# Attention with a bias over 1024 positions: in steps with 3, 5 or 7 key blocks, the smaller group of blocks is worked first

## The reference

```python
x = x + layer0(x)   # attention: LN, q and k normalised, relative position bias, causal, null key
x = x + layer1(x)   # attention: LN, a given bias (16, 1024, 1024), key mask, causal, null key
x = x + moe2(x)     # 8 experts, top 2, and a shared expert
x = x + moe3(x)
# an attention layer, with b=2, n=1024, 16 heads of 64, one shared k and v for all heads:
sim  = q @ k.T + bias               # (b, h, n, n+1), causal and key mask applied
attn = softmax(sim)
out  = LN((attn @ v) @ Wout)        # 1024 -> 256
```

## Time and profile before

| what | value |
|---|---|
| median of 3 runs | 1618.56 us |
| the profiled execution | 1616.94 us |
| its span | 1615.1 us |
| TensorE matmul busy | 1434.6 us (89%) |
| VectorE busy | 1398.2 us (87%) |
| ScalarE busy | 1168.1 us (72%) |
| GpSimd busy | 903.7 us (56%) |
| the six steps T2, T4, T6, T10, T12, T14 | 74.8, 86.8, 93.4, 62.3, 75.9, 89.8 us |

### The profile page before, as it was taken

How to read it: one execution, slowest core, us unless ns; L and a number is a source line. 1 busy time by engine, 2 the same in 40 slices (tenths; PEclk the granted TensorE clock), 3 DMA queues, 4 the chain that set the end, 5 groups by cost and what they waited for, 6 DMA issues and landing times.

```text
span 1615.1 us, 45627 instructions
## 1 busy us (share of the span) xinstructions
PE 1434.6 (89%) x15680; PEld 1069.2 (66%) x15680; DVE 1398.2 (87%) x3629; ACT 1168.1 (72%) x3093; POOL 903.7 (56%) x1766
## 2 busy tenths in 40 slices
PE   4677778888999999977788999999999989999998
PEld 2455556666777777855666777777878756666665
DVE  6667888899999999977789998999999889888887
ACT  4566778888989999967788898989999633333332
POOL 6666778776756556577665344444343366632222
PEclk8789999999999999999999999999999999999999
DMA  6002211112222134012122122212223000000000
GB/s 158 18 28 69 71 48 54 60 67 73 80 87 93 48 107 131 9 47 67 54 61 79 60 75 87 84 68 88 100 106 106 2 27 20 1 1 1 14 14 27
DMA packets 49954, 96.50 MB, mean 60 GB/s; under 512 B 2922, under 2 KB 26560, under 8 KB 49728
## 3 DMA queue, kind: packets, MB, share of 16 engines
q1 hardware_dynamic: 48420, 92.93, 17.7%
q10 hardware_dynamic: 1308, 0.67, 0.2%
HBM read 91.41 MB, written 2.17 MB: 58 GB/s over the span
## 4 chain that ended last, share of the span: by engine, by line
PE 57%; DVE 20%; ACT 7%; issue 7%; POOL 4%; DVEq 0%; ACTq 0%; POOLq 0%
PE tp L1787 10%; DVE biased L1253 6%; PE sc L1655 6%; DVE p_lo L1351 5%; PE sc L1445 4%; PE sc L1447 4%; PE sc L1446 4%; PE sc L1656 4%; DVE q_a L1285 3%; PE aux L1445 3%; PE op L1445 3%; PE aux L1447 2%; PE aux L1446 2%; PE op L1447 2%; PE op L1446 2%
## 5 line engine op out<-in xcount | busy, mean ns | idle before, releaser
L1351 DVE TENSOR_TENSOR p_lo<-tp,p_hi 128x256 f16<-128x256 f32 (+3 forms) x896 | 424.8, 496 | 78.8 <-ACT p_hi L932 70.0
L1787 PE MATMUL tp<-ident,probs 128*128 128x128 f32 x2304 | 414.7, 280 | 24.6 <-DVE p_lo L1351 20.3
L932 ACT ACTIVATE p_hi<-tp 128x256 f16<-128x256 f32 (+3 forms) x896 | 385.2, 445 | 39.4 <-PE tp L1787 26.3
L832 ACT ACTIVATE probs<-biased,neg_max 128x256 f32<-128x256 f32 (+7 forms) x512 | 396.2, 774 | 14.7 <-DVE neg_max L1253 12.9
L1445 PE MATMUL op<-v_s,p_hi 128*128 128x64 f16 x2304 | 297.6, 194 | 28.2 <-DVE p_lo L1351 18.9
L1655 PE MATMUL sc<-k_a,q_a 128*128 128x512 f16 (+3 forms) x768 | 254.1, 331 | 65.9 <-DVE neg_max L1253 50.7
L1787 PEld LDWEIGHTS tp<-ident,probs 128*128 128x128 f32 x2304 | 261.6, 142 | 67.5 <-issue 29.0
L1446 PE MATMUL op<-v_s,p_hi 128*128 128x64 f16 x2304 | 297.2, 193 | 0.0
L1447 PE MATMUL op<-v_s,p_lo 128*128 128x64 f16 x2304 | 297.2, 193 | 0.0
L1445 PEld LDWEIGHTS op<-v_s,p_hi 128*128 128x128 f16 x2304 | 219.7, 99 | 47.7 <-DVE p_lo L1351 30.8
L1656 PE MATMUL sc<-k_b,q_b 128*128 128x512 f16 (+3 forms) x768 | 242.0, 329 | 0.0
(11 more groups left out here) (354 smaller groups left out, 3617.9 us busy)
## 6 DMA issues: line engine op xcount, KB each, us to landing
bias<-rel_table SPq DMA_DIRECT2D x4, 2048.0 KB, 9.1
bias<-in_fside_16xSxS SPq DMA_DIRECT2D x4, 2048.0 KB, 8.1
bias<-rel_table SPq DMA_DIRECT2D x4, 1792.0 KB, 7.3
bias<-in_fside_16xSxS SPq DMA_DIRECT2D x4, 1792.0 KB, 7.3
bias<-rel_table SPq DMA_DIRECT2D x4, 1536.0 KB, 6.2
bias<-in_fside_16xSxS SPq DMA_DIRECT2D x4, 1536.0 KB, 6.5
bias<-rel_table SPq DMA_DIRECT2D x4, 1280.0 KB, 5.6
bias<-in_fside_16xSxS SPq DMA_DIRECT2D x4, 1280.0 KB, 6.5
```

The lines of the kernel that those rows point to most:

```text
L832: ac.activation(probs[:, i % 2, 0:w], biased[:, i % 2, 0:w], ACT.Exp, bias=neg_max[:, u % 2, i % HU:i % HU + 1], scale=-1.0, accum_out=row ...
L932: ac.activation(p_hi[:, gi % 4, 0:nb * P], tp[gi % 2][:, 0:nb * P], ACT.Copy)\
L1351: ve.tensor_tensor(p_lo[:, gi % 4, 0:nb * P], tp[gi % 2][:, 0:nb * P], p_hi[:, gi % 4, 0:nb * P], ALU.subtract).then_inc(s["p_lo"], 1)
L1787: last = te.transpose(tp[gi % 2][:, jj * P:(jj + 1) * P], probs[:, n % 2, (j0 + jj) * P:(j0 + jj + 1) * P], ident[:, :])
```

## The change

The plan of groups changes in one expression. For an odd number nk of blocks, group A had (nk + 1) / 2 blocks and group B the rest; now A has nk // 2 blocks and B has one more. For an even nk both forms give the same, and one or two blocks stay one group.

```diff
-            first = nk if nk <= 2 else (nk + 1) // 2
+            first = nk if nk <= 2 else nk // 2
```

## The result

The changed kernel takes 1620.08 us, the median of 20 runs (1618.68 to 1624.24), against 1617.35 us for the kernel before, again of 20 runs (1615.99 to 1621.14). The ratio is 1.0018 with a 95% interval of 1.0013 to 1.0024: **0.18% slower, 2.7 us**. The forecast was 1615.2 us, 0.21% faster. The result lies inside the range and, as forecast, within 0.3%, but on the other side of no change, and the interval excludes a gain. The reasons were wrong in at least one term, and the rest of this document finds it.

What follows compares the result with a forecast made beforehand. Waits were taken to bound three blocks, nearly full TensorE or VectorE the five and seven. Terms -3.15, -0.6 and +0.4 gave -3.35 us: 1613.6 from the profiled 1616.94, expected median 1615.2, range 1609 to 1621.

Steps and rivals of the forecast that it cites:

- T10: Step with three blocks: five of eight units counted as plain, each gaining 0.35 us; 1.75 us faster.
- T2: Step with three blocks: four of eight units counted as plain, each gaining 0.35 us; 1.4 us faster.
- T12: Step with five blocks: work at k2 starts 0.10 us earlier per unit; at most 0.8 us, 0.6 taken as gain.
- T4: Step with five blocks, VectorE 92% busy: no change, taken as 0.
- T6 and T14: Steps with seven blocks: B 0.16 us later in 16 units, mostly hidden; 0.4 us slower together.
- What bounds the kernel: Three blocks: a loop of waits in T10; five: TensorE in T12, VectorE in T4; seven: TensorE in T14, both in T6.
- Seven blocks: In slot k1, B ends 0.16 us later, hidden by TensorE's backlog; cost 0 to 2.6 us, 0.4 taken.
- Three blocks, k1 to k2: A(k2) turned 0.25 us earlier, `p_hi` of B ends 0.35 earlier; 0.35 us won per plain unit.
- Three blocks, k0: Start of a unit: stall moves from A to B, B through at 828.16 instead of 828.27; 0.11 us won.
- Five blocks: At k2 of T12 the ScalarE row starts 0.10 us earlier per unit, 0.6 us won; T4 0.
- The wait only moves: Rival: A's waits become B's, the loop closing through B's unmoved end; 0 within 1 us, 1618.5 us, chance 0.25.
- Large last groups delay the scores: Rival: later end of B(k1) delays row maximum and scores; 5.8 us slower, 1624.4 us, chance 0.14.

Runs made afterwards that it cites:

- the experiment with k1 alone: Smaller group first only in slots k1 of the steps with five and seven blocks, against the kernel before: 1620.46 us, ratio 1.0015.
- the added load: Two unused VectorE statistics added ending slot k1, third and eighth units of T2 to T15: 1622.97 us on the kernel before, 1626.21 us on the changed kernel.
- three blocks alone: Smaller group first only in the steps with three blocks, against the kernel before: 1618.36 us against 1617.44, ratio 1.0004.

## Why the prediction was wrong, by its steps

| term | predicted | by units | by steps |
|---|---|---|---|
| T10 | -1.75 | -0.33 | 0.0 |
| T2 | -1.4 | +0.15 | +0.2 |
| T12 | -0.6 | +0.41 | +0.6 |
| T4 | 0 | +0.30 | +0.4 |
| T6 and T14 | +0.4 | +1.47 | +1.6 |
| sum | -3.35 | +2.0 | +2.8 |

By units the forecast was off by 5.4 us: 3.0 in the steps with three blocks, 1.3 in those with five, 1.1 in those with seven. The sign of the result comes from the five and seven blocks, the larger part of the miss from the three.

**What bounds the kernel: half right.** The three kinds of step were read correctly, but "TensorE is 98% busy" was taken to mean that TensorE sets T14. It doesn't set the first two units of T14, which lost most: there the chain goes from B's `p_lo` over VectorE's further work and the maximum to the scores, with 0.33 us of idle TensorE behind it (the unit that lost, above), though TensorE is 98% busy over the step.

**Seven blocks: the cover that wasn't there.** The price was right to a hundredth, 0.16 us for the end of B(k1) against 0.15 measured. So was the place. What failed is "what hides it is TensorE's own backlog", and with it 0.4 out of a bound of 2.6. The row for it was a share over a whole step; the row that would have told was one wait in one unit, the scores' wait of 0.33 us for the row maximum. An engine with idle time ahead of the very instruction that is delayed has no backlog there. Measured are 1.5 us by units, more than half of the bound. The spacing that the 0.16 rested on was right too: the products start 0.03 us apart in the rows above (1102.02, 1102.05, 1102.08). The Trainium skill ("TensorE: Matmul & The Clock Gate", section "Back-to-back issue gap") gives about 81 ns a matmul for 128 columns. Taken over to these products, which have 64, as the prediction did to see what would follow, it would have let the delay vanish; this trace shows 0.03 us for them, and the delay came.

**Three blocks, k1 to k2: the mechanism right, the count wrong.** A plain unit of T10 won 0.33, 0.30 and 0.34 us where 0.35 had been worked out, and the inner steps came within 0.02 (0.23 for 0.25, 0.43 for 0.43). But there are three plain units in T10, not five, and the units that I costed at nothing lose 0.05 to 0.18 each. 3 x 0.33 = 1.0 won, 0.64 lost. "Not every unit is plain" was used to leave units out of the gain, and should have been followed by what the change does in them. In the first unit of T10 the argument of the seven blocks applies word for word: the statistics stand behind B(k1), which ends 0.14 us later, and the unit is 0.14 longer. In T2, where four units at 0.35 had been counted, four win 0.81 together and three lose 0.95.

**Three blocks, k0: wrong.** The 0.11 us from "through at 828.16 instead of 828.27" went nowhere. The scores of the next unit start at a constant distance from the end of B(k3), 0.68 us in T10 and 1.21 in T14, before and after alike; VectorE does the row maximum they need right behind that `p_lo`. Nor is TensorE ready 0.11 earlier. The sum ended with the turning of B(k0) and left out what follows it, the product of B(k3), which now has a block more (0.085 us). In the rows of T10 above, the last product before the scores starts 0.56 us after B(k3) before (820.79) and 0.54 after (824.33), and TensorE idles for that difference. The rows print no wait there, since the times of the matmuls overlap (0.19 us each, 0.03 apart): the distance from the last product's start to the scores shows it.

**Five blocks: wrong sign.** The wait for `q_a` fell in T12 from 3.3 to 3.0 us, half of the 0.6 I took, and the step grew by 0.6. Of the eight units only the eighth gained clearly (-.16; the third -.04), and by the experiment with k1 alone (-.20 there) it comes from k1, not from k2 where the prediction had it. Six units lose 0.09 to 0.14, as in T14.

**The rivals.** "The wait only moves" was right for three blocks as a sum, though for another reason, gains and losses that cancel. "Large last groups delay the scores" had the mechanism, the place and the sign, and got 0.14; its size of 5.8 us was twice the measured 2.7, because it charged every unit, and in plain units the maximum has slack (0.4 us in the third of T14, as the added load showed) or a gain in another slot cancels the delay. Its condition, "as soon as the maximum comes later than TensorE does", was the right one to look up unit by unit, and the signs named for it didn't all show: T6 and T14 grew by 1.6 us, while the scores' wait in T14 grew only from 0.7 to 1.0. What stays open is the exact account of the plain units with seven blocks, where k1 and the other slots cancel, and of T2, whose gains and losses repeat unit by unit with three blocks alone but were not traced to their waits.

## What to carry to other kernels

When a change makes one item of a pipeline end later, don't look for cover in the step's busy shares: go to the instruction that is delayed and read whether the engine behind it idles just ahead of the next one, and do so in each kind of unit, not in the plainest. A unit left out of the gain must still be put through the loss. In this kernel, with two groups passed over three engines, no order that ran beat near equal groups with the odd block in the first, since the next row of work hangs on the end of the second group; for three blocks alone the order made no difference that could be measured.

## What the runs showed of the hardware

Two `p_lo` back to back took 1.16 us for 4 + 3 blocks, and 0.56 + 0.69 = 1.25 us with an idle time between them: apart, the pair keeps VectorE busy for 0.09 us more, which no count of instructions shows. Short instructions cost far more than their columns: with 8 of 256 columns, 3% of the data, L1405 still took 159 of 418 ns and L1409 284 of 405. And one profile's span can be off by nearly 2 us in a step without any change (T0), while the unchanged units of T10 to T15 repeat to one to three hundredths.
